# Pruned attention: five of the eight slots of VectorE hand copy 2 to ScalarE

## The chip, the cores and the metric

The kernel runs on one core of one Trainium2 chip. The time is the device time of one execution in microseconds (us), with all inputs in HBM. The core has a matrix engine (TensorE, PE), a vector engine (VectorE, DVE), a scalar engine (ScalarE, ACT), a general one (GpSimd, POOL) and one that here only issues DMAs (SyncE, SP). Each runs its own instructions in the order in which they are written; they meet through semaphores only.

## What is computed

A decoder of two layers on 8 sequences of 512 tokens with 256 features. Of its six parts the change concerns one, the cross-attention of layer 0, with 16 heads of 16 features. Its columns of scores are pruned: for each head the probabilities are summed over the queries, and only the 460 key positions with the largest sums are kept.

```python
scores = jnp.einsum('bhqd,bhkd->bhqk', q, k) / math.sqrt(D_K)
scores = jax.nn.softmax(scores, axis=-1)
keep = int(S * PRUNE_KEEP)
col_sum = jnp.sum(scores, axis=2)
_, idx = jax.lax.top_k(col_sum, keep)
mask = jnp.zeros((B, H, S), scores.dtype).at[jnp.arange(B)[:, None, None], jnp.arange(H)[None, :, None], idx].set(1.0)
pruned = scores * mask[:, :, None, :]
return jnp.einsum('bhqk,bhkd->bhqd', pruned, v)
```

## The kernel before

The program is a sequence of stages; `stage_xattn0` is the pruned attention. It goes through 8 batches `b`, each in two halves `u` of 8 heads, and through a half in 8 slots `h` = 0 to 7, one head in each (`slots`). Batches 0 and 1 are written out, batches 2 to 7 are a loop, so that each engine jumps back five times; a last pass (b = 8) ends the pipeline. Heads are counted by `n`.

In slot `h` of head n the engines do this, in the order of their code:

- PE: transposes 0 of head n-2 (`turn`, L911), the second half of the scores of head n (`scores`, L903), transposes 1, then what the slot has besides (value products of the half before in slots 0 to 5, L892; output projection in slots 6 and 7 of halves with u = 1, L957; the turned column sums in slot 3, L940), transposes 2, the first half of the scores of head n+1, transposes 3.
- DVE: the maximum of score rows for two of the four row tiles (`maxima`, L795), the reciprocal of the row sums of head n-1 (L791), the maxima of the other two, its copies, and between them the search for the 52 smallest column sums of the half before. The search has 16 steps (`search`: L808, L818, L826, L811), three in each of slots 3 to 7 and one more in slot 7, and works on 8 partitions, one per head. In slot 0 DVE prunes the values (`xa_vm`, L855), in slots 0 to 2 with u = 0 it does the layer norm of an earlier batch (L832 to L840 and L879).
- ACT: copy 0 of head n-2, two exponentials with row sums (L764), copy 1, two more exponentials, copy 3. In slot 6 it first copies a result, `xa_oT` (L772).
- POOL: the normalisation of head n (L746), four operations, after the reciprocal.

A copy (`turned`, L668 to L681) takes one transposed 128 x 512 tile of probabilities from PSUM (`xa_ps_t`) to SBUF (`xa_probT`) and sums it along its row, which gives the column sum. A head has four tiles t = 0 to 3. `by_vector` says which engine copies tile t in slot h: DVE on L679 with a `tensor_scalar`, ACT on L681 with an `activation`, each with an accumulator as second output, read by an instruction of its own. Before, DVE has tile 2 in all slots and tile 3 in slot 1: 9 of 32 copies in a half.

PSUM has two buffers for transposes, `ps_t[t % 2]`. So `turn` makes PE wait until an earlier copy has freed one: transposes 2 and 3 wait for copies 0 and 1 of the same slot, transposes 0 and 1 for copies 2 and 3 of the slot before.

Of the kernel before, what the change touches and what calls it, by code (L numbers as in the profile page):

```python
# [56 lines left out]
def wait(eng, sem, count):  # L57

    if not isinstance(count, int) or count > 0:
        eng.wait_ge(sem, count)  # L60
# [520 lines left out]
def stage_xattn0(nc, a):  # L581
# [16 lines left out]
    with ExitStack() as ctx:  # L598
# [38 lines left out]
        def since(b, first):  # L637
            return not isinstance(b, int) or b >= first

        def batches(eng, body):  # L640

            body(0)
            body(1)
            with eng.Fori(2, B) as b:
                body(b)
            body(B)

        def slots(b):
            for u in range(2):
                for h in range(HU):  # L650
                    yield u, h, HU * u + h, 2 * HU * b + HU * u + h, not isinstance(b, int) or b < B
# [5 lines left out]
        def has_before2(b, u):  # L657
            return not isinstance(b, int) or 2 <= 2 * b + u <= 2 * B + 1

        def by_vector(h, t):  # L660

            return t == 2 or (t == 3 and h == 1)

        def turning(b, u, h, n, real):

# [92 lines left out]
        @block.scalar  # L758
        def _(act):
            def body(b):  # L760
                def exponentials(h, n, j):
                    act.wait_ge(max_up, 2 * n + j + 1)
                    for t in (2 * j, 2 * j + 1):
                        ins = act.activation(probs[h % NP][:, t, :], ps_s[j][:, t % 2, :], ACT.Exp,  # L764
                                             bias=nmax[h % 2][:, t:t + 1], accum_out=rsum[h % 2][:, t:t + 1])
                    ins.then_inc(exp_up, 1)

                for u, h, hh, n, real in slots(b):
                    if h == 6 and has_before2(b, u):
                        act.wait_ge(vals_up, 2 * b + u - 1)  # L770
                        wait(act, y_up, 2 * (b - 1))
                        act.activation(oT[:, u, :], ps_v[:, :], ACT.Copy).then_inc(oT_up, 1)  # L772
                    turned(act, b, u, h, n, real, 0)
                    if real:
                        wait(act, t_up, 4 * (n - 3))
                        exponentials(h, n, 0)
                    turned(act, b, u, h, n, real, 1)
                    if real:
                        exponentials(h, n, 1)
                    if not by_vector(h, 3):  # L780
                        turned(act, b, u, h, n, real, 3)
            batches(act, body)

        @block.vector
        def _(dve):
# [56 lines left out]
            def body(b):  # L842
                for u, h, hh, n, real in slots(b):
                    if real:
                        maxima(n, h, 0)
                    search(b, u, h, (0,))
                    if (real or (u, h) == (0, 0)) and not (isinstance(b, int) and n == 0):
                        reciprocal(n - 1, h - 1)
                    if real:
                        maxima(n, h, 1)  # L850
                    if h == 0 and has_before2(b, u):
                        dve.wait_ge(kept_up, 2 * b + u - 1)
                        dve.wait_ge(v_ld[u], 16 * b)
                        for q4 in range(2):
                            ins = dve.tensor_tensor(vm[:, :, q4, :, q4 * DK:(q4 + 1) * DK],  # L855
                                                    v[u][:, :, q4 * QH * DK:(q4 + 1) * QH * DK].rearrange("p t (j d) -> p t j d", d=DK),
                                                    ps_m[:, 0:T * HU].rearrange("p (t q j o) -> p t q j o", t=T, q=2, o=1)[:, :, q4, :, :]
                                                    .to_broadcast([P, T, QH, DK]), ALU.mult)
                        ins.then_inc(vm_up, 1)
                    search(b, u, h, (1,))  # L860
                    turned(dve, b, u, h, n, real, 2)
                    if by_vector(h, 3):
                        turned(dve, b, u, h, n, real, 3)
                    search(b, u, h, (2, 3) if h == HU - 1 else (2,))
                    if u == 1 and h in (6, 7) and since(b, 1):
                        i = h - 6
                        dve.wait_ge(y_up, 2 * b - 1 + i)
                        dve.wait_ge(xb_up, b)
                        dve.tensor_tensor(x_in[:, 2 * i:2 * i + 2, :], ps_m[:, :].rearrange("p (t d) -> p t d", t=2),
                                          x_in[:, 2 * i:2 * i + 2, :], ALU.add).then_inc(add_up, 1)  # L870
                    if (u, h) == (0, 0) and since(b, 2):
                        stats(b - 2)
                    if (u, h) == (0, 2) and since(b, 2):
                        finish(b - 2)
# [1545 lines left out]
```

## Time and profile before

| | us |
|---|---|
| time, median of 3 runs (2188.01 to 2202.6) | 2197.36 |
| the profiled execution's own time | 2182.38 |
| its span, first to last instruction | 2180.6 |
| PE busy in the span | 1880.1 (86%) |
| DVE busy | 1300.3 (60%) |
| ACT busy | 959.1 (44%) |
| POOL busy | 609.9 (28%) |

The profile is that of one execution. A row of a timeline has the start of an instruction in us from the span's start, how long it lasted, engine, line, operation and operands; in brackets stands the idle time of the engine before it and what ended it ("issue": nothing that the profile shows). Rows of one engine can overlap a little at their ends, so the time that an operation occupies is read from the start of it to the start of the next one, when the engine does not wait between. The pruned attention lies between about 325 and 1010 us.

### The profile page before, as it was taken

What the parts mean: (1) busy time and instruction counts of PE and PEld (TensorE: products, weight loads), DVE (VectorE), ACT (ScalarE), POOL (GpSimd) and SP (SyncE); (2) the same over time, 40 slices, a digit from 0 to 9 for tenths busy, and PEclk for the clock granted to TensorE, in tenths of its full rate; (3) what the DMA queues carried; (4) which work ended last, traced back from release to release, by engine and by line L of the source; (5) the groups of instructions that cost most, each with busy time, mean ns of one, the idle gap of its engine ahead of it and who ended that gap; (6) DMA issues with size and microseconds to landing.
All of it is one profiled execution on the core that took longest, in us unless ns stands there. A gap on an engine that the chain in (4) does not pass through costs nothing. (4 is left out here: it accounts for less than half of the span.)

```text
span 2180.6 us, 28641 instructions
## 1 busy us (share of the span) xinstructions
PE 1880.1 (86%) x8625; PEld 1134.5 (52%) x8625; DVE 1300.3 (60%) x3113; ACT 959.1 (44%) x2451; POOL 609.9 (28%) x781
## 2 busy tenths in 40 slices
PE   7794857888888888884697899999879999999997
PEld 5452534444554454551565565666555656566553
DVE  2483437988988988983354121122266677766655
ACT  3231549988888888880232211111123232223220
POOL 2010005555555555551355000100143122211100
PEclk9897988999999999997666999999999999999999
DMA  5523752112112112202622333433321121100000
GB/s 193 231 87 99 248 183 65 46 54 67 56 54 66 55 54 60 61 20 73 203 92 91 98 109 132 138 123 130 107 77 59 34 63 44 30 15 25 10 10 20
DMA packets 166839, 184.51 MB, mean 85 GB/s; under 512 B 19620, under 2 KB 145819, under 8 KB 165696
## 3 DMA queue, kind: packets, MB, share of 16 engines
q1 hardware_dynamic: 159424, 158.57, 22.5%
q0 software_dynamic: 6144, 16.18, 2.4%
q10 hardware_dynamic: 1152, 8.39, 0.9%
q8 instruction: 48, 0.79, 0.2%
q14 instruction: 71, 0.58, 0.1%
HBM read 118.68 MB, written 58.72 MB: 81 GB/s over the span
## 5 line engine op out<-in xcount | busy, mean ns | idle before, releaser
L746 POOL TENSOR_SCALAR xa_probs<-xa_probs,xa_rinv 128x512 f32<-128x512 f32 x512 | 344.6, 692 | 294.6 <-DVE xa_rinv L791 294.6
L911 PE MATMUL xa_ps_t<-xa_ident,xa_probs 128*128 128x128 f32 x2048 | 325.7, 285 | 60.8 <-POOL xa_probs L746 55.0
L764 ACT ACTIVATE xa_probs<-xa_ps_s,xa_nmax 128x512 f32<-128x512 f32 x512 | 351.9, 708 | 25.8 <-DVE xa_nmax L795 25.4
L911 PEld LDWEIGHTS xa_ps_t<-xa_ident,xa_probs 128*128 128x128 f32 x2048 | 232.4, 143 | 240.1 <-POOL xa_probs L746 84.7
L795 DVE TENSOR_REDUCE xa_nmax<-xa_ps_s 128x2 f32<-128x1024 f32 x256 | 307.3, 1201 | 39.5 <-PE xa_ps_s L903 38.0
L681 ACT ACTIVATE xa_probT<-xa_ps_t 128x512 f32<-128x512 f32 x368 | 226.5, 621 | 63.0 <-PE xa_ps_t L911 54.1
L2268 PE MATMUL ta_ps_e<-k_ew,ta_x5T 128*128 128x512 f32 x512 | 244.2, 613 | 1.5 <-DVE ta_acc L2018 1.4
L903 PE MATMUL xa_ps_s<-xa_k,xa_q 96*128 96x512 bf16 x512 | 157.8, 391 | 54.9 <-ACT xa_probs L764 34.5
L2018 DVE SCALAR_TENSOR_TENSOR ta_acc<-ta_ps_e,ta_gate,ta_acc 128x256 f32<-128x256 f32 x256 | 123.5, 482 | 101.7 <-PE ta_ps_e L2268 95.5
L1459 ACT ACTIVATE ex_hid<-ex_ps_g 128x512 f32<-128x512 f32 x64 | 38.2, 598 | 274.1 <-PE ex_ps_u L1561 274.1
L1515 DVE TENSOR_TENSOR ex_hid<-ex_hid,ex_ps_u 128x512 f32<-128x512 f32 x64 | 44.0, 687 | 182.0 <-ACT ex_hid L1459 182.0
L2268 PEld LDWEIGHTS ta_ps_e<-k_ew,ta_x5T 128*128 128x128 f32 x512 | 98.4, 197 | 102.7 <-issue 86.5
L892 PE MATMUL xa_ps_v<-xa_probT,xa_vm 128*32 128x512 f32 x1024 | 135.2, 619 | 0.8 <-DVE xa_vm L855 0.8
L679 DVE TENSOR_SCALAR_CACHE_REDUCE xa_probT<-xa_ps_t 128x512 f32<-128x512 f32 x144 | 97.7, 679 | 41.4 <-PE xa_ps_t L911 40.0
L1561 PE MATMUL ex_ps_g<-ex_xsT,k_wg 128*128 128x512 f32 x256 | 120.4, 592 | 2.1 <-ACT ex_xsT L1441 2.1
L1561 PE MATMUL ex_ps_u<-ex_xsT,k_wu 128*128 128x512 f32 x256 | 120.3, 592 | 0.0
L764 ACT ACTIVATION_READ_ACCUMULATOR xa_probs<-xa_ps_s,xa_nmax 128x1 f32 x512 | 116.7, 228 | 0.0
L1571 PE MATMUL ex_ps_d<-k_wd,ex_hid 128*128 128x256 f32 x512 | 113.4, 379 | 0.1
L1571 PEld LDWEIGHTS ex_ps_d<-k_wd,ex_hid 128*128 128x128 f32 x512 | 96.0, 190 | 13.3 <-DVE ex_hid L1515 0.5
L903 PEld LDWEIGHTS xa_ps_s<-xa_k,xa_q 96*128 96x128 bf16 x512 | 45.0, 100 | 77.2 <-ACT xa_probs L764 49.8
L681 ACT ACTIVATION_READ_ACCUMULATOR xa_probT<-xa_ps_t 128x1 f32 x368 | 84.7, 230 | 0.0
L1183 POOL DMA_INDIRECT scratch_buf<-ro_xs,ro_pi x64 | 63.0, 984 | 67.8 <-issue 67.8
(356 smaller groups left out, 2935.2 us busy)
## 6 DMA issues: line engine op xcount, KB each, us to landing
xa_q<-scratch_qk_parts SPq DMA_DIRECT2D x192, 64.0 KB, 2.2
xa_k<-scratch_qk_parts SPq DMA_DIRECT2D x192, 64.0 KB, 2.2
scratch_buf<-rec_zeros ACTq DMA_DIRECT2D x8, 1024.0 KB, 12.0
k_wg<-in_L_ffn_Wg SPq DMA_DIRECT2D x16, 512.0 KB, 5.8
k_wu<-in_L_ffn_Wu SPq DMA_DIRECT2D x16, 512.0 KB, 6.0
k_wd<-in_L_ffn_Wd SPq DMA_DIRECT2D x16, 512.0 KB, 6.7
ex_xs<-scratch_buf SPq DMA_DIRECT2D x16, 512.0 KB, 4.9
scratch_results<-ex_out SPq DMA_DIRECT2D x16, 512.0 KB, 3.3
```

The source lines that it names most:

```text
L679: eng.tensor_scalar(dst, src, 1.0, 0.0, ALU.mult, ALU.add, accum_out=out).then_inc(copied[t], 1)
L681: eng.activation(dst, src, ACT.Copy, accum_out=out).then_inc(copied[t], 1)
L746: ins = pool.tensor_scalar(probs[h % NP][:, t, :], probs[h % NP][:, t, :], rinv[h % 2][:, t:t + 1], 1.0, ALU.mult, ALU.mult)
L764: ins = act.activation(probs[h % NP][:, t, :], ps_s[j][:, t % 2, :], ACT.Exp, bias=nmax[h % 2][:, t:t + 1], accum_out=rsum[h % 2][:, t:t + 1])
L795: dve.tensor_reduce(nmax[h % 2][:, 2 * j:2 * j + 2], ps_s[j][:, :, :], AX.X, ALU.max, negate=True).then_inc(max_up, 1)
L892: ins = pe.matmul(ps_v[32 * j:32 * j + 32, :], vm[:, t, four, j, :], probT[u][:, QH * four + j, t, :], start=(four == 0 and t == 0), stop= ...
L903: ins = pe.matmul(ps_s[j][:, t % 2, :], q[c % 2][:, hh % CH, t * P:(t + 1) * P], k[c % 2][:, hh % CH, :], start=True, stop=True)
L911: ins = pe.transpose(ps_t[t % 2][:, i * P:(i + 1) * P], probs[(h - 2) % NP][:, i, t * P:(t + 1) * P], ident[:, :])
L1561: ins = pe.matmul(ps[:, :], wt[:, h, j * P:(j + 1) * P], xsT[u][:, h, :], start=(h == 0), stop=(h == DH - 1))
L1571: ins = pe.matmul(ps_d[:, t, :], hid[u][:, j, t * P:(t + 1) * P], wd[u][:, j, :], start=(j == 0), stop=(j == FT - 1))
L2018: dve.scalar_tensor_tensor(acc[c % 2][:, t, :], ps_e[n % 2][:, i, :], gate[c % 2][:, t, e:e + 1], acc[c % 2][:, t, :], ALU.mult, ALU.add). ...
L2268: ins = pe.matmul(ps_e[n % 2][:, :, :].rearrange("p e d -> p (e d)"), x5T[c % 2][:, h, t * P:(t + 1) * P], ew[:, h, e:e + 2, :].rearrange( ...
```

## The change

`by_vector` gets another rule: DVE copies tile 2 in slots 0, 1 and 2, and tile 3 in slots 1 and 2, which are 5 of 32 copies in a half; ACT copies the other 27. In code, both engines now ask the rule for tiles 2 and 3 at the places where their copies 2 and 3 stood. All arithmetic and all buffers stay.

```diff
--- before.py
+++ after.py
@@ -659,7 +659,7 @@
 
         def by_vector(h, t):
 
-            return t == 2 or (t == 3 and h == 1)
+            return h < 3 and (t == 2 or (t == 3 and h > 0))
 
         def turning(b, u, h, n, real):
 
@@ -777,8 +777,9 @@
                     turned(act, b, u, h, n, real, 1)
                     if real:
                         exponentials(h, n, 1)
-                    if not by_vector(h, 3):
-                        turned(act, b, u, h, n, real, 3)
+                    for t in (2, 3):
+                        if not by_vector(h, t):
+                            turned(act, b, u, h, n, real, t)
             batches(act, body)
 
         @block.vector
@@ -858,9 +859,9 @@
                                                     .to_broadcast([P, T, QH, DK]), ALU.mult)
                         ins.then_inc(vm_up, 1)
                     search(b, u, h, (1,))
-                    turned(dve, b, u, h, n, real, 2)
-                    if by_vector(h, 3):
-                        turned(dve, b, u, h, n, real, 3)
+                    for t in (2, 3):
+                        if by_vector(h, t):
+                            turned(dve, b, u, h, n, real, t)
                     search(b, u, h, (2, 3) if h == HU - 1 else (2,))
                     if u == 1 and h in (6, 7) and since(b, 1):
                         i = h - 6
```

On ACT, the excerpt runs from slot 5 to slot 7 of a half with an `xa_oT` copy (names: `xa_probT` the copies, `xa_probs` the exponentials). Before:

```order
L764 ACTIVATE xa_probs,xa_rsum<-xa_ps_s,xa_nmax 128x512 x2
L681 ACTIVATE xa_probT,xa_colsum<-xa_ps_t 128x512
L772 ACTIVATE xa_oT<-xa_ps_v 128x512
L681 ACTIVATE xa_probT,xa_colsum<-xa_ps_t 128x512
L764 ACTIVATE xa_probs,xa_rsum<-xa_ps_s,xa_nmax 128x512 x2
L681 ACTIVATE xa_probT,xa_colsum<-xa_ps_t 128x512
L764 ACTIVATE xa_probs,xa_rsum<-xa_ps_s,xa_nmax 128x512 x2
L681 ACTIVATE xa_probT,xa_colsum<-xa_ps_t 128x512 x2
L764 ACTIVATE xa_probs,xa_rsum<-xa_ps_s,xa_nmax 128x512 x2
```

The same place in the changed kernel:

```order
L764 ACTIVATE xa_probs,xa_rsum<-xa_ps_s,xa_nmax 128x512 x2
L681 ACTIVATE xa_probT,xa_colsum<-xa_ps_t 128x512 x2
L772 ACTIVATE xa_oT<-xa_ps_v 128x512
L681 ACTIVATE xa_probT,xa_colsum<-xa_ps_t 128x512
L764 ACTIVATE xa_probs,xa_rsum<-xa_ps_s,xa_nmax 128x512 x2
L681 ACTIVATE xa_probT,xa_colsum<-xa_ps_t 128x512
L764 ACTIVATE xa_probs,xa_rsum<-xa_ps_s,xa_nmax 128x512 x2
L681 ACTIVATE xa_probT,xa_colsum<-xa_ps_t 128x512 x3
L764 ACTIVATE xa_probs,xa_rsum<-xa_ps_s,xa_nmax 128x512 x2
```

The two copies in a row (3, then 0 of the next slot) have become three (2, 3, then 0), and the one before `xa_oT` has become two.

On DVE, the excerpt runs from the copies of slot 1 to the search step after the copy of slot 3 (L795 and L796 are maxima, L791 and L792 reciprocals, `xa_left` and `xa_m` the search). Before:

```order
L679 TENSOR_SCALAR xa_probT,xa_colsum<-xa_ps_t 128x512 x2
L795 TENSOR_REDUCE xa_nmax<-xa_ps_s 128x2
L791 RECIPROCAL xa_rinv<-xa_rsum 128x4
L795 TENSOR_REDUCE xa_nmax<-xa_ps_s 128x2
L679 TENSOR_SCALAR xa_probT,xa_colsum<-xa_ps_t 128x512
L795 TENSOR_REDUCE xa_nmax<-xa_ps_s 128x2
L808 TENSOR_SCALAR xa_left<-xa_ps_m 8x512
L791 RECIPROCAL xa_rinv<-xa_rsum 128x4
L795 TENSOR_REDUCE xa_nmax<-xa_ps_s 128x2
L818 MAX xa_m<-xa_left 8x8
L679 TENSOR_SCALAR xa_probT,xa_colsum<-xa_ps_t 128x512
L826 MATCH_REPLACE xa_left<-xa_m,xa_left 8x512
```

And in the changed kernel:

```order
L679 TENSOR_SCALAR xa_probT,xa_colsum<-xa_ps_t 128x512 x2
L796 TENSOR_REDUCE xa_nmax<-xa_ps_s 128x2
L792 RECIPROCAL xa_rinv<-xa_rsum 128x4
L796 TENSOR_REDUCE xa_nmax<-xa_ps_s 128x2
L679 TENSOR_SCALAR xa_probT,xa_colsum<-xa_ps_t 128x512 x2
L796 TENSOR_REDUCE xa_nmax<-xa_ps_s 128x2
L809 TENSOR_SCALAR xa_left<-xa_ps_m 8x512
L792 RECIPROCAL xa_rinv<-xa_rsum 128x4
L796 TENSOR_REDUCE xa_nmax<-xa_ps_s 128x2
L819 MAX xa_m<-xa_left 8x8
L827 MATCH_REPLACE xa_left<-xa_m,xa_left 8x512
```

Slot 2 has two copies instead of one, and the copy between the search steps of slot 3 is gone, as it is in slots 4 to 7.

## Rows read from the trace of the kernel before

**Rows 1.** The page's 40 slices of 54.5 us: busy share in tenths.
```profile
DVE  2483437988988988983354121122266677766655
ACT  3231549988888888880232211111123232223220
```

**Rows 2.** Windows: busy us (count) of PE, PEld, DVE, ACT, POOL; PEclk; DMA.
```profile
380.00:390.00 10.00, 8.14 (x43) 5.67 (x44) 10.00 (x21) 9.27 (x30) 5.38 (x8) 0.83 0.11 33
640.00:720.00 80.00, 68.67 (x469) 38.73 (x468) 72.75 (x147) 69.96 (x217) 45.16 (x65) 1.00 0.20 60
```

**Rows 3.** The page's costliest groups: count | busy us, mean ns | idle before.
```profile
L681 ACT ACTIVATE xa_probT<-xa_ps_t 128x512 f32<-128x512 f32 x368 | 226.5, 621 | 63.0 <-PE xa_ps_t L911 54.1
...
L679 DVE TENSOR_SCALAR_CACHE_REDUCE xa_probT<-xa_ps_t 128x512 f32<-128x512 f32 x144 | 97.7, 679 | 41.4 <-PE xa_ps_t L911 40.0
```

**Rows 4.** Timeline of ACT, slots 4 to 7 of a half with u=1.
```profile
707.55 0.60 ACT L681 ACTIVATE xa_probT<-xa_ps_t 128x512 f32<-128x512 f32 x1 [0.47 <-PE xa_ps_t L911]
...
712.55 0.60 ACT L681 ACTIVATE xa_probT<-xa_ps_t 128x512 f32<-128x512 f32 x1 [0.48 <-PE xa_ps_t L911]
...
716.93 0.63 ACT L772 ACTIVATE xa_oT<-xa_ps_v 128x512 f32<-128x512 f32 x1
717.40 0.64 ACT L681 ACTIVATE xa_probT<-xa_ps_t 128x512 f32<-128x512 f32 x1
...
724.62 0.59 ACT L681 ACTIVATE xa_probT<-xa_ps_t 128x512 f32<-128x512 f32 x1
...
726.51 0.61 ACT L681 ACTIVATE xa_probT<-xa_ps_t 128x512 f32<-128x512 f32 x1
...
728.83 0.60 ACT L681 ACTIVATE xa_probT<-xa_ps_t 128x512 f32<-128x512 f32 x1 [1.61 <-issue]
```

**Rows 5.** Timeline of PE, the same slots: transposes after POOL and after ACT.
```profile
711.86 0.66 PE L911 MATMUL xa_ps_t<-xa_ident,xa_probs 128*128 128x128 f32 x4 [1.00 <-POOL xa_probs L746]
...
725.35 0.66 PE L911 MATMUL xa_ps_t<-xa_ident,xa_probs 128*128 128x128 f32 x4 [0.39 <-ACT xa_probT L681]
```

**Rows 6.** Timeline of DVE: slots 1, 2 and 4 with u=0; slot 3 with u=1.
```profile
655.03 0.69 DVE L679 TENSOR_SCALAR_CACHE_REDUCE xa_probT<-xa_ps_t 128x512 f32<-128x512 f32 x1 [1.00 <-PE xa_ps_t L911]
...
655.90 0.69 DVE L679 TENSOR_SCALAR_CACHE_REDUCE xa_probT<-xa_ps_t 128x512 f32<-128x512 f32 x1 [0.17 <-PE xa_ps_t L911]
...
660.55 1.38 DVE L879 TENSOR_SCALAR xa_x_in<-xa_x_in,xa_mv,xa_rstd 128x256 f32<-128x256 f32 x4
...
666.64 1.20 DVE L795 TENSOR_REDUCE xa_nmax<-xa_ps_s 128x2 f32<-128x1024 f32 x1
...
670.22 0.67 DVE L679 TENSOR_SCALAR_CACHE_REDUCE xa_probT<-xa_ps_t 128x512 f32<-128x512 f32 x1
...
670.83 0.68 DVE L818 MAX8 xa_m<-xa_left 8x8 f32<-8x512 f32 x1
671.43 1.19 DVE L795 TENSOR_REDUCE xa_nmax<-xa_ps_s 128x2 f32<-128x1024 f32 x1
...
703.14 0.68 DVE L808 TENSOR_SCALAR xa_left<-xa_ps_m 8x512 f32<-8x512 f32 x1 [0.88 <-PE xa_ps_m L940]
```

**Rows 7.** Timeline of ACT, a half with u=0, and slot 0 after it.
```profile
663.10 0.69 ACT L764 ACTIVATE xa_probs<-xa_ps_s,xa_nmax 128x512 f32<-128x512 f32 x1 [0.52 <-DVE xa_nmax L795]
...
667.38 0.60 ACT L681 ACTIVATE xa_probT<-xa_ps_t 128x512 f32<-128x512 f32 x1 [0.34 <-PE xa_ps_t L911]
...
686.65 0.60 ACT L681 ACTIVATE xa_probT<-xa_ps_t 128x512 f32<-128x512 f32 x1 [0.33 <-PE xa_ps_t L911]
...
687.85 0.69 ACT L764 ACTIVATE xa_probs<-xa_ps_s,xa_nmax 128x512 f32<-128x512 f32 x1 [0.52 <-DVE xa_nmax L795]
```

**Rows 8.** Timeline of ACT in the stage's first half: slots 6 and 7.
```profile
353.11 0.74 ACT L681 ACTIVATE xa_probT<-xa_ps_t 128x512 f32<-128x512 f32 x1
...
353.68 0.84 ACT L764 ACTIVATE xa_probs<-xa_ps_s,xa_nmax 128x512 f32<-128x512 f32 x1
...
358.04 0.89 ACT L764 ACTIVATE xa_probs<-xa_ps_s,xa_nmax 128x512 f32<-128x512 f32 x1
```

## The prediction

> **What bounds the kernel now.** I read the slices first: VectorE (DVE) and ScalarE (ACT) are both at eight or nine tenths from slice 8 to 18 [rows 1]. That is the pruned attention, and nothing outside it is touched. The windows view of 80 us in its middle has DVE busy 72.8, ACT 70.0 and TensorE (PE) 68.7 us [rows 2]: three engines near their limit, so sums over the stage decide nothing, and the timeline has to be read slot by slot (a slot is one head; "slot 3" is h = 3).
>
> In slots 3 to 7 DVE has no idle time. Its first maximum of one slot starts at 666.64 and that of the next at 671.43, 4.79 us later, and the copy between them is handed over without a gap (copy at 670.22, search step at 670.83) [rows 6]. ACT runs after it: from copy 0 of slot 4 (707.55) to that of slot 5 (712.55) it needs 5.00 us, of which 0.48 is idle time before the copy, ended by PE's transposes [rows 4], which had themselves waited 1.00 us for GpSimd (POOL), and this for DVE's reciprocal [rows 5]. With no search, as in the stage's first half, the same seven ACT operations repeat after 4.36 us (353.68 to 358.04) [rows 8]. So in slots 3 to 7 DVE sets a pace of 4.79, and ACT could do 4.36.
>
> **Prices of one operation.** A copy on ACT, back to back with what follows, occupies 0.57 us (353.11 to 353.68) [rows 8], though such a row lasts 0.60 and more; so an exponential is (4.36 - 3 x 0.57) / 4 = 0.66 [rows 8]. A copy on DVE occupies 0.61 (670.22 to 670.83) [rows 6]. A copy is thus equally dear on both, and only place and order matter.
>
> **What the change moves.** In slots 3 to 7 copy 2 goes from DVE to ACT, in slot 2 copy 3 goes the other way: net 4 of 32 per half, 64 in the 16 halves, so ACT's 368 copies become 432 and DVE's 144 become 80 [rows 3]. Nothing is removed or added; PE, POOL and the DMA queues keep their order.
>
> *Slots 3 to 7, DVE.* 4.79 - 0.61 = 4.18 us of work: no longer the limit.
>
> *Slots 3 to 7, ACT.* Four exponentials and four copies: 4 x 0.66 + 4 x 0.57 = 4.92 us, already over 4.79. Then comes a wait that is new. PE writes transposes 0 and 2 of a head into the same PSUM buffer, so the next slot's transposes 0 wait for copy 2. Copy 2 is now ACT's last but one operation. An ACT copy releases PE 0.73 after its start (copy at 724.62 [rows 4], transposes waiting for it at 725.35 [rows 5]), and ACT starts a copy 0.69 after its transposes start (711.86 [rows 5] to 712.55 [rows 4]): 1.42 us from copy 2 to the next copy 0, while copies 2 and 3 fill 1.14. So 0.28 us of idle time, and a slot of **5.20 us**. Queued behind copy 0 are the exponentials, for which DVE's reciprocal and POOL wait; they had some 1.9 us to spare, as DVE now comes to the reciprocal early.
>
> *From copy 0 of slot 4 to copy 0 of slot 0.* Half with u = 0: 667.38 to 686.65, 19.27 us [rows 7]. After: four slots of 5.20, and in slot 6 the copy of oT (0.47: 716.93 to 717.40 [rows 4]), which covers the 0.28, so +0.20: 21.0. **+1.7**. Half with u = 1: 707.55 to 728.83, 21.28 us [rows 4]. After: 5.20 + 5.40 + 5.20 and a last slot of 4.92 plus what ACT needs from the start of its last copy to the new loop pass, less that copy's own 0.57 (2.32 - 0.57 = 1.75; "issue", 726.51 to 728.83 [rows 4]), which hides the 0.28: 22.5. **+1.2**.
>
> *Slot 3.* DVE has to do copy 3 of slot 2 before the first maximum of slot 3. Two copies in a row start 0.87 apart (655.03, 655.90), since PE has to turn in between; so DVE is free 0.87 later than at 660.55 [rows 6]. In a half with u = 0 this delays the exponential of 663.10, which waits for the maximum, to 663.97 [rows 7]; 3.21 later (four exponentials and a copy) copy 2 starts, 1.42 later the next copy 0: 668.60 instead of 667.38. **+1.2**. With u = 1 DVE has 0.88 idle at 703.14 for the column sums [rows 6], which takes this up; there the sum is **+0.3** (the same working without the four DVE operations of L879 in front). What ACT saves in slot 2 (0.57) ends in this wait.
>
> *Slot 0 after a half with u = 0.* ACT waited 0.52 for a maximum (687.85), DVE being late from its search [rows 7]. Gone: **-0.6**, with the propagation.
>
> Slots 0 to 2 otherwise stay: PE is full there with the value matmuls.
>
> **The sum.** Per batch 1.7 + 1.2 + 1.2 + 0.3 - 0.6 = 3.8. Batches 1 to 7: 26.6, less 0.9 because batch 1 has no L879 in front. First half of batch 0, ACT-bound at 4.36: 5 x (5.20 - 4.36) = 4.2. Second half of batch 0: about 1.5. Together **+31 us**. The profiled execution took 2182.4, so 2213; it lies below all three timed ones (2188.0 to 2202.6), so against their median of 2197.4 I predict **2228 us**. What a measurement of this kernel can tell from no change is about 1%, 22 us.
>
> **A page against the trace.** The rows give 0.57 per ACT copy with its accumulator [rows 8]. The Trainium skill, page "ScalarE: Activation LUTs", section "What ACT_TABLE_LOAD costs", gives an ACTIVATE with immediate scale 186 ns + 0.833 ns per element and lets neighbours overlap by about 93 ns: an estimate of 0.52 for 512 elements. By that, four copies would take 0.2 less per slot, and the time would grow by about 15 us instead of 31. The trace disagrees, and the measured 0.57 stands; that formula has no accumulator read-out. The same page's section "Rules for kernel authors" sends multiplications to VectorE, not ScalarE, for its speed in bf16; these are fp32 tiles in PSUM, and the rows show 0.61 against 0.57.
>
> **The rivals.**
>
> *The 0.28 wait does not come* (PE turns sooner than its rows say, or runs ahead). Slots of 4.92: seven waits of 0.28 fewer per batch, 13.7, and 2.8 in batch 0: +15, 2212. For it: PE has over 1 us to spare in these slots. Against: the 1.42 is made of two measured steps with no slack in them. Chance 0.14.
>
> *Copies in a row are cheaper on ACT.* The oT copy, which reads no accumulator, occupies 0.47 [rows 4]. If the three copies in a row went at that pitch, a slot would be 4 x 0.66 + 4 x 0.47 = 4.52 plus a wait of 1.42 - 0.94 = 0.48, so 5.00 for 5.20: 0.2 less in 5 x 16 slots, +15, again 2212. Chance 0.05. (The Trainium skill's formula above points this way.)
>
> *Faster.* Only if that pitch held and the wait were gone too would ACT's 4.52 beat the 4.79 of now, by 0.27 x 5 x 15 = 20 us: 2177. It decides below a slot of 4.79. Against both: copies 3 and 0 already run back to back in the first half, at 4.36 per slot [rows 8], which leaves no such saving. Chance 0.04.
>
> *PE's clock.* It is granted 1.00 from 640 to 720 with PE busy 0.86, but 0.83 from 380 to 390, where PE is busy 0.81 [rows 2]. Slots of 5.20 leave PE idle more. If each of the 14 later halves lost one further 1 us to a spell at the lower level (1.2 GHz), the time would be 2242. It points the same way as the forecast. Chance 0.15.
>
> *The forecast:* ACT takes over as the bound, 0.28 wait included. Chance 0.62.
>
> **How the numbers follow.** Slower by over 1% means above 2219: the forecast and the clock (0.77), less a little for the spread of the runs: 0.75. Within 1%: the first two rivals (0.19), which may also end a little above: 0.20. Faster: 0.05. The range goes from 2207 (first rival, less 5 for spread) to 2246 (clock, plus 4).
>
> **What would show it.** ACT: in slots 3 to 6 copy 0 starts every 5.20, with 0.2 to 0.3 idle before it, ended by PE, and PE's transposes waiting there for ACT's copy instead of POOL. DVE: idle before its second maximum, and 80 copies. Stage about 31 us longer, nothing else moved. Wrong if slots 4 to 7 repeat in 4.9 or less, if DVE still has no gaps there, or if the loss sits in slots 0 to 2.

## The result and the profile after

The changed kernel took 2257.98 us in the median (2249.07 to 2265.07), the kernel before 2193.01 us beside it: a ratio of 1.0297, 95% interval 1.0252 to 1.0341. It is slower by 65 us, where 31 were predicted.

The page of the changed kernel, its slices and the groups that answer to [rows 1] and [rows 3]:

```profile
PE   7785857788787888786389699999978999999997
...
DVE  2482436877777787777144212122256776666655
ACT  3232648988887888885033211111113322223220
...
PEclk9897978998999999999676699999989999999999
...
L764 ACT ACTIVATE xa_probs<-xa_ps_s,xa_nmax 128x512 f32<-128x512 f32 x512 | 349.8, 700 | 43.9 <-DVE xa_nmax L796 43.7
L681 ACT ACTIVATE xa_probT<-xa_ps_t 128x512 f32<-128x512 f32 x432 | 261.7, 618 | 69.6 <-PE xa_ps_t L912 68.8
...
L679 DVE TENSOR_SCALAR_CACHE_REDUCE xa_probT<-xa_ps_t 128x512 f32<-128x512 f32 x80 | 55.1, 690 | 47.7 <-PE xa_ps_t L912 47.7
```

ACT has its 432 copies and DVE its 80, as counted. DVE's eights and nines of before are sevens, ACT's stayed at eight: nobody is full, and yet it takes longer. Over 420 to 1000 us the windows view has PE (the first number after the stretch's length) busy for less time than before, and a lower granted clock (the third number from the end). Before, and then in the changed kernel:

```profile
420.00:1000.00 580.00, 492.74 (x3326) 280.27 (x3326) 521.86 (x1060) 492.02 (x1513) 318.88 (x452) 0.98 0.18 55
...
420.00:1000.00 580.00, 470.87 (x3049) 269.69 (x3048) 460.01 (x862) 492.99 (x1522) 294.50 (x421) 0.94 0.17 53
```

The span grew from 2180.6 to 2252.9 us. From the first exponential of the stage to its last one it is 647.5 us before and 713.9 after (327.18 to 974.68, and 328.43 to 1042.31): 66 of the 72 us lie there.

The timeline of ACT in slots 3 to 5 of a half with u = 0, which answers to [rows 4]:

```profile
705.98 0.62 ACT L681 ACTIVATE xa_probT<-xa_ps_t 128x512 f32<-128x512 f32 x1
...
706.55 0.63 ACT L681 ACTIVATE xa_probT<-xa_ps_t 128x512 f32<-128x512 f32 x1
...
707.50 0.60 ACT L681 ACTIVATE xa_probT<-xa_ps_t 128x512 f32<-128x512 f32 x1 [0.23 <-PE xa_ps_t L912]
...
711.30 0.62 ACT L681 ACTIVATE xa_probT<-xa_ps_t 128x512 f32<-128x512 f32 x1
...
712.82 0.60 ACT L681 ACTIVATE xa_probT<-xa_ps_t 128x512 f32<-128x512 f32 x1 [0.23 <-PE xa_ps_t L912]
```

and PE at the same place:

```profile
706.83 0.63 PE L912 MATMUL xa_ps_t<-xa_ident,xa_probs 128*128 128x128 f32 x4 [1.35 <-ACT xa_probT L681]
```

The mechanism is the predicted one. Copy 2 starts at 705.98, copy 3 at 706.55, PE's next transposes have waited 1.35 us for ACT and not for POOL, and copy 0 comes at 707.50; the next pair is 711.30 and 712.82. From copy 2 to copy 0 it is 1.52 us, where 1.42 was predicted, and a slot takes 5.33 (707.50 to 712.82) and not 5.20.

But look at the loop end, where DVE's operations of [rows 6] would have followed each other without a gap:

```profile
770.17 0.67 DVE L870 TENSOR_TENSOR xa_x_in<-xa_ps_m,xa_x_in 128x512 f32<-128x512 f32 x1
773.44 1.23 DVE L796 TENSOR_REDUCE xa_nmax<-xa_ps_s 128x2 f32<-128x1024 f32 x1 [2.60 <-issue]
775.75 0.18 DVE L792 RECIPROCAL xa_rinv<-xa_rsum 128x4 f32<-128x4 f32 x1 [1.08 <-issue]
```

ACT at the same place:

```profile
771.47 0.60 ACT L681 ACTIVATE xa_probT<-xa_ps_t 128x512 f32<-128x512 f32 x1 [0.17 <-PE xa_ps_t L912]
...
774.70 0.69 ACT L764 ACTIVATE xa_probs<-xa_ps_s,xa_nmax 128x512 f32<-128x512 f32 x1 [2.55 <-DVE xa_nmax L796]
...
777.11 0.69 ACT L764 ACTIVATE xa_probs<-xa_ps_s,xa_nmax 128x512 f32<-128x512 f32 x1 [0.38 <-DVE xa_nmax L796]
```

and PE (L893 are the value products):

```profile
776.20 0.61 PE L904 MATMUL xa_ps_s<-xa_k,xa_q 96*128 96x512 bf16 x2 [2.98 <-ACT xa_probs L764]
...
777.86 1.93 PE L893 MATMUL xa_ps_v<-xa_probT,xa_vm 128*32 128x512 f32 x8 [0.37 <-DVE xa_vm L856]
```

DVE stands still for 2.60 us and again for 1.08, and the profile shows nothing that it waits for. ACT waits 2.55 us for DVE's maximum, PE 2.98 us for ACT, and eight value products take 1.93 us in place of the 1.06 that they take otherwise: after this idle time the granted clock falls (0.57 from 777 to 781 us). The prediction had no such row: before, it was ACT that stood still at this place, 1.61 us [rows 4]. The waits view of DVE from 680 to 960 us lists four of each, one pair at each loop end.

For the rest of this text a **step** is the time from the first exponential of one slot to that of the next, read from ACT's timeline. These are the steps of batch 5, which is in the loop; the last one of the second row crosses the loop end. "Placed" is the changed kernel with DVE's code moved (below), "early" ACT's copy 2 between the exponentials.

| | h = 0 | 1 | 2 | 3 | 4 | 5 | 6 | 7 | sum |
|---|---|---|---|---|---|---|---|---|---|
| before, u = 0 | 5.70 | 5.01 | 5.04 | 4.86 | 4.79 | 4.85 | 4.78 | 5.47 | 40.5 |
| before, u = 1 | 4.94 | 5.76 | 4.36 | 5.22 | 5.01 | 4.83 | 5.30 | 6.27 | 41.7 |
| changed, u = 0 | 6.91 | 5.60 | 5.93 | 5.33 | 5.58 | 5.41 | 5.39 | 5.33 | 45.5 |
| changed, u = 1 | 4.93 | 5.77 | 4.64 | 5.33 | 5.33 | 5.40 | 5.39 | 7.94 | 44.7 |
| changed, placed, u = 0 | 5.60 | 5.10 | 5.92 | 5.34 | 5.33 | 5.41 | 5.86 | 5.33 | 43.9 |
| changed, placed, u = 1 | 4.94 | 5.77 | 4.63 | 5.34 | 5.33 | 5.41 | 5.41 | 5.27 | 42.1 |
| slots 3 to 7 only, early, u = 0 | 5.56 | 5.30 | 5.03 | 4.94 | 4.93 | 5.40 | 5.30 | 4.93 | 41.4 |
| slots 3 to 7 only, early, u = 1 | 4.99 | 5.77 | 4.35 | 5.23 | 5.01 | 5.40 | 4.92 | 4.96 | 40.6 |

The changed kernel has three kinds of loss: slots 3 to 6 at 5.3 to 5.4 and slot 2 at 5.9 or 4.6, which were predicted; 7.94 and 6.91 around the loop end, which were not; and single steps in other halves, such as 7.22 and 7.18 in slot 0 of batches 1 and 2 with u = 1, where 4.94 is usual. They turn out to be the clock's.

### The profile page after: what moved, and what is told of

The parts are those of the page before. It is cut to its first block and busy times, and to the rows that moved or that the text cites. A ratio compares the mean times of both kernels' runs of the same rounds, so it can differ in the third digit from the quotient of the medians.

```text
span 2252.9 us, 28641 instructions
## 1 busy us (share of the span) xinstructions
PE 1905.7 (85%) x8625; PEld 1158.6 (51%) x8625; DVE 1275.0 (57%) x2985; ACT 999.4 (44%) x2579; POOL 609.9 (27%) x781
## 5 line engine op out<-in xcount | busy, mean ns | idle before, releaser
L912 PE MATMUL xa_ps_t<-xa_ident,xa_probs 128*128 128x128 f32 x2048 | 338.0, 295 | 96.5 <-ACT xa_probT L681 95.3
L912 PEld LDWEIGHTS xa_ps_t<-xa_ident,xa_probs 128*128 128x128 f32 x2048 | 247.1, 149 | 279.1 <-issue 159.7
L796 DVE TENSOR_REDUCE xa_nmax<-xa_ps_s 128x2 f32<-128x1024 f32 x256 | 310.6, 1214 | 112.0 <-PE xa_ps_s L904 96.5
L764 ACT ACTIVATE xa_probs<-xa_ps_s,xa_nmax 128x512 f32<-128x512 f32 x512 | 349.8, 700 | 43.9 <-DVE xa_nmax L796 43.7
L681 ACT ACTIVATE xa_probT<-xa_ps_t 128x512 f32<-128x512 f32 x432 | 261.7, 618 | 69.6 <-PE xa_ps_t L912 68.8
L904 PE MATMUL xa_ps_s<-xa_k,xa_q 96*128 96x512 bf16 x512 | 167.8, 412 | 61.6 <-ACT xa_probs L764 41.5
L893 PE MATMUL xa_ps_v<-xa_probT,xa_vm 128*32 128x512 f32 x1024 | 141.9, 647 | 2.6 <-DVE xa_vm L856 2.6
L681 ACT ACTIVATION_READ_ACCUMULATOR xa_probT<-xa_ps_t 128x1 f32 x432 | 97.9, 227 | 0.0
L679 DVE TENSOR_SCALAR_CACHE_REDUCE xa_probT<-xa_ps_t 128x512 f32<-128x512 f32 x80 | 55.1, 690 | 47.7 <-PE xa_ps_t L912 47.7
```

The lines of the kernel that those rows point to most:

```text
L681: eng.activation(dst, src, ACT.Copy, accum_out=out).then_inc(copied[t], 1)
L796: dve.tensor_reduce(nmax[h % 2][:, 2 * j:2 * j + 2], ps_s[j][:, :, :], AX.X, ALU.max, negate=True).then_inc(max_up, 1)
L893: ins = pe.matmul(ps_v[32 * j:32 * j + 32, :], vm[:, t, four, j, :], probT[u][:, QH * four + j, t, :], start=(four == 0 and t == 0), stop= ...
L904: ins = pe.matmul(ps_s[j][:, t % 2, :], q[c % 2][:, hh % CH, t * P:(t + 1) * P], k[c % 2][:, hh % CH, :], start=True, stop=True)
L912: ins = pe.transpose(ps_t[t % 2][:, i * P:(i + 1) * P], probs[(h - 2) % NP][:, i, t * P:(t + 1) * P], ident[:, :])
```

## The experiments

Ratios are to the kernel before, run beside each.

### The loop end

**DVE without a loop, in the changed kernel.**

```diff
-            batches(dve, body)
+            for b in range(B + 1):
+                body(b)
             stats(B - 1)
```

> The changed kernel, but with VectorE's part of the pruned attention written out for all batches instead of looped from batch 2; the other engines keep their loops, and every operation and its order stay. Theory A (the relief of VectorE uncovers its own loop jump: 2.60 us of VectorE idle at each loop end of the changed kernel, 0 before, and PE's clock falls after it): the jump goes, the step from slot 7 to slot 0 falls from 7.9 to about 5.6 us and the one after it from 6.9 to about 5.6, some 3.5 us for each of 5 loop ends, so 17 us less than the changed kernel, a ratio to the kernel before of about 1.022. Rival B (that idle time is only where some other engine's jump shows): no change, ratio 1.029 to 1.030.

Measured: 2232.11 us, ratio 1.0188 (1.0150 to 1.0225), so some 24 us less than the changed kernel, where 17 were expected. The step across the loop end fell from 7.9 to 5.26, the next from 6.9 to 5.55. The loss at the loop end is DVE's.

**The same in the kernel before.**

> The kernel before with the same edit, as the control. Theory A: VectorE's jump was covered by its backlog of queued work, so nothing is gained: ratio 0.998 to 1.002. Rival B2 (written-out code is quicker for reasons of its own, or slower to fetch): a change like that of the other kernel, some 15 us in either direction.

Measured: 2192.03 us, ratio 0.9992 (0.9967 to 1.0016). Written-out code gains nothing as such. Up to here my theory was that DVE always lost this time at the jump and had hidden it behind its backlog.

**Only slots 3 to 7 moved,** slot 2 as before.

```diff
-            return h < 3 and (t == 2 or (t == 3 and h > 0))
+            return h < 3 and (t == 2 or (t == 3 and h == 1))
```

> Only the first part of the change: copy 2 to ScalarE in slots 3 to 7; copy 3 of slot 2 stays on ScalarE. Theory (VectorE's extra copy in slot 2 delays the first maximum of slot 3 by 0.9 us where the layer norm's four operations stand before it, little elsewhere): about 1 us less per batch than the changed kernel, 6 to 8 us, a ratio of about 1.026. Rival (the extra copy is covered by PE, which is full there): ratio as the changed kernel's, 1.029 to 1.030, or above it as ScalarE has 0.57 more to do.

Measured: 2224.52 us, ratio 1.0149 (1.0112 to 1.0186): 33 us less than the changed kernel, where 6 to 8 were expected, and this is what overthrew the theory. Slot 2 gave its 0.9 (5.03 for 5.93), but the loop end also went from 7.9 to 5.27, and DVE's waits "issue" were gone, though its loop was still a loop and it had even less to do. The view of the DMA queues told why. From 680 to 960 us the changed kernel has on its instruction queue

```profile
q1 hardware_dynamic: 18285, 14.46, 17.0%
q14 instruction: 17, 0.14, 0.2%
```

17 fetches of 8 KB (0.14 MB over 17), and the kernel before

```profile
q1 hardware_dynamic: 19344, 15.22, 18.2%
q14 instruction: 16, 0.13, 0.2%
```

16 of them. Four of the changed kernel's fall at each loop end, and one in mid-pass. The kernel with slots 3 to 7 moved has none at all. So some loops are not fetched again after their first pass, and some are fetched anew in each. In the kernel before it was ACT's loop; in the changed one, whose two loops have other lengths and starts, ACT's stays and DVE's does not.

**DVE's loop moved by 16 instructions,** in the changed kernel. The 16 memsets go to a tile of their own and are executed once, while DVE waits for the stage to begin.

```diff
+            for i in range(16):
+                dve.memset(spare[:, i:i + 1], 0.0)
             dve.wait_ge(pad_up, 1)
```

> The changed kernel with 16 tiny VectorE memsets into an unused tile at the start of the pruned attention, before VectorE's loop; nothing in the loop is changed. In the changed kernel four 8 KB fetches of instructions fall at each loop end and one in mid-pass, and VectorE stands idle for them; in the one with only slots 3 to 7 moved there is none at all, though VectorE has as much idle time. Theory P (whether VectorE's loop stays in its instruction buffer depends on where its code lies, not on how busy it is): shifting the loop by 16 instructions takes it out of the bad place: no fetches in the loop, steps from slot 7 to 0 of 5.3 instead of 7.9 and from 0 to 1 of 5.6 instead of 6.9, ratio about 1.019. Theory A (the loop jump shows because VectorE has no backlog): no change, 1.029.

Measured: 2236.24 us, ratio 1.0179 (1.0114 to 1.0244). Sixteen instructions more, and 26 us less than the changed kernel (1.0297 - 1.0179). The size is loose: the two intervals allow 9 to 43 us, and the medians differ by 22. The traces are sharper. The two steps around a loop end take 10.88 us together at each of the five, where the changed kernel takes 14.8 to 15.1: 20 us in all, and the stage from its first to its last exponential is 24 us shorter (689.9 for 713.9). Its queues from 680 to 960 us; there is no row for an instruction queue:

```profile
## 3 DMA queue, kind: packets, MB, share of 16 engines
q1 hardware_dynamic: 19872, 16.00, 18.7%
issues: line engine op xcount, KB each, median us to landing
```

**By 64, and by 128.** Each was executed once.

> The same with 64 memsets. Theory P: fetches in the loop either there or not, depending on the place; with both this and the one of 16 unlike the changed kernel, place is the cause. Theory A: the same fetches and the same idle time of 2.6 us at each loop end as in the changed kernel, a time of about 2258.

> The changed kernel with 128 memsets ahead of VectorE's loop, which is 8 KB of instructions at 64 bytes each, the size of one fetch. Theory P128 (what counts is where in such a block the loop begins and ends): the place is as bad as in the changed kernel: fetches in the loop, 15 to 17 of them from 680 to 960, steps of 7.9 and 6.9 at the loop end, and a time of about 2258. Rival (the place counts in some other way, by distance from something else): no fetches, 2232 to 2238, as with 16 and 64.

With 64: 2232.54 us, no fetches, steps of 5.27 across the loop end. With 128: 2250.72 us, and the queues again have

```profile
q1 hardware_dynamic: 18207, 14.40, 17.2%
q14 instruction: 17, 0.14, 0.2%
```

with DVE idle for its maximum four times and for its reciprocal four times:

```profile
DVE xa_nmax L799 <- issue: 10.4, 4, 2.7
DVE xa_rinv L795 <- issue: 4.4, 4, 1.1
```

Over the whole span this kernel has one packet more on that queue than the changed kernel (73 for 72), so 128 instructions are about the 8 KB of one fetch. A shift by 16 or 64 cures, a shift by 128 restores the fault, steps of 7.9 and 6.9 included. These three shifts fit the reading that what decides is where the loop's code lies within such a block; other shifts were not tried. The Trainium skill, page "Runtime: NRT & Kernel Launch", section "Instruction fetch mechanics", describes a small instruction buffer that is refilled in order, and a stall where a jump's target is not in it. The trace agrees with the stall, 2.60 us of it in DVE's row at 773.44; the page's refill unit is 16 KB, while the packets here are of 8 KB, and 8 KB is the shift that brings the fault back. (A second instruction queue, q8, does have packets of 16 KB: 48 packets, 0.79 MB in every run; in the changed kernel none of them falls from 600 to 960 us.) Which start and which length are bad was not worked out.

**ACT's loop moved by 40 instructions,** in the kernel before.

```diff
+            for i in range(40):
+                apart(act, past_act)
```

> The kernel before with 40 semaphore increments put ahead of ScalarE's first pass of the pruned attention; its loop is unchanged, only moved. In the kernel before, ScalarE stands idle 1.6 to 1.8 us at each loop end and 16 fetches of instructions fall in the stretch from 680 to 960. Theory P (place of a loop in the instruction stream decides on fetches, on this engine too): if the new place is a good one, no fetch in that stretch and 0.9 us less per loop end, the rest being covered by VectorE's backlog: 4 to 5 us less, ratio 0.998. If nothing changes, either the place is bad too or the theory does not hold for ScalarE.

Measured: 2187.06 us, ratio 0.9981 (0.9960 to 1.0002). The fetches are gone,

```profile
## 3 DMA queue, kind: packets, MB, share of 16 engines
q1 hardware_dynamic: 19344, 15.22, 18.0%
issues: line engine op xcount, KB each, median us to landing
```

and so are ACT's waits "issue", which shows the same for a second engine. The time fell by about 4 us, the size expected, but the interval holds 1, and the trace does not bear out the 0.9 us per loop end. The two steps around a loop end take 11.84 us together at each of the five, and in the kernel before they take 11.83 or 11.84 at three of them, with ACT's fetches there: DVE's load is the bound, and the fetches cost nothing. The other two took 12.77 and 12.06 before, with the granted clock at 0.73 and 0.72 just after; whether ACT's fetches had a part in that is not shown.

### The slots

**Copy 2 early.** In the changed kernel, ACT does copy 2 between its last two exponentials (`between()` executes it there, in the slots in which it is ACT's).

```diff
                     for t in (2 * j, 2 * j + 1):
+                        if t == 3:
+                            between()
```

> The changed kernel with ScalarE's copy 2 of slots 3 to 7 done between the last two exponentials instead of after them, so that two operations lie between it and the next copy 0 instead of one. Theory W (in slots 3 to 7 the pace is ScalarE's work of 4.92 us plus a wait for PE, which waited for copy 2): slots fall from 5.33 to about 4.92 to 4.95, 0.4 in 7 slots of each of 8 batches, about 23 us less than the changed kernel, a ratio of about 1.019; if the shorter slots uncover other waits, less. Rival (the wait is bound by something else, such as the clock or the reciprocal): slots stay above 5.2 and the ratio above 1.026.

Measured: 2227.37 us, ratio 1.0161 (1.0125 to 1.0196). ACT's timeline in slots 3 and 4:

```profile
690.01 0.67 ACT L681 ACTIVATE xa_probT<-xa_ps_t 128x512 f32<-128x512 f32 x1
...
690.58 0.77 ACT L766 ACTIVATE xa_probs<-xa_ps_s,xa_nmax 128x512 f32<-128x512 f32 x1
...
691.24 0.68 ACT L681 ACTIVATE xa_probT<-xa_ps_t 128x512 f32<-128x512 f32 x1
...
691.81 0.69 ACT L681 ACTIVATE xa_probT<-xa_ps_t 128x512 f32<-128x512 f32 x1
...
692.38 0.79 ACT L766 ACTIVATE xa_probs<-xa_ps_s,xa_nmax 128x512 f32<-128x512 f32 x1
```

Copy 2 at 690.01, an exponential, copies 3 and 0 at 691.24 and 691.81 without a gap. PE's transposes, waiting for copy 2, start

```profile
690.91 0.63 PE L917 MATMUL xa_ps_t<-xa_ident,xa_probs 128*128 128x128 f32 x4 [0.68 <-ACT xa_probT L681]
```

0.90 after it, and their result is there when ACT comes to it. Slots 3, 4, 6 and 7 mostly fell to 4.93 to 4.95 (4.92 by ACT's work alone; 5.01 in slot 4 with u = 1). So 0.4 us of each of these slots was this wait. The step of slot 5, in which the copy to `xa_oT` stands between copy 2 and the next copy 0, stayed at 5.41: there the wait had been covered, as predicted. The total fell by 30 us where 23 were expected; the time at the lower clock fell too, from 66 to 41 us between 420 and 1000. The loop end kept its 7.9, DVE's code being that of the changed kernel.

**Copy 2 early and slot 2 as before.** This is the kernel with only slots 3 to 7 moved, with the copy between the exponentials; neither loop is fetched anew.

> Copy 2 to ScalarE in slots 3 to 7 as in the change, but placed between the last two exponentials, and slot 2 left as before. By ScalarE's work alone: slots of 4.93 and one of 5.41 against 4.79 to 5.0 before, no wait for copy 2, no extra copy ahead of slot 3, and no fetches in the loop (both loops lie as in the kernel with only slots 3 to 7 moved). Per batch about 1.0 more than before in slots 3 to 7 and 0.9 less at the loop end: ratio 0.999 to 1.004. If the overload of ScalarE costs more than its own work says, 1.008 or above.

Measured: 2189.18 us, ratio 0.9982 (0.9964 to 1.0000). ACT's waits from 420 to 960 us in this kernel:

```profile
ACT xa_probT L681 <- PE xa_ps_t L917: 26.3, 26, 1.9
ACT xa_probs L766 <- DVE xa_nmax L801: 5.4, 12, 0.5
```

and in the changed kernel, for the same stretch:

```profile
ACT xa_probT L681 <- PE xa_ps_t L912: 50.0, 77, 3.1
ACT xa_probs L764 <- DVE xa_nmax L796: 29.6, 24, 2.7
```

All of the move to ACT in slots 3 to 7, and no loss, also against the kernel before with ACT's loop moved (0.9981), which likewise fetches neither loop anew. The overload of ACT as such (4.92 against 4.79 in a slot) is paid back in halves with u = 1 (40.6 for 41.7), where DVE was the slower one.

**Slot 2 alone:** copy 3 of slot 2 to DVE, the rest as before.

```diff
+            return t == 2 or (t == 3 and h in (1, 2))
```

> Only the second part of the change: copy 3 of slot 2 goes to VectorE, while copy 2 of slots 3 to 7 stays there. Working from the slot steps: with u = 0 the first maximum of slot 3 comes 0.87 us later and, VectorE being without gaps until slot 7, that delay is not made up: about 0.9 per batch; with u = 1 some 0.3. So 8 us, ratio 1.003 to 1.005, if the loop fetches stay as before; up to 20 us more (1.013) if VectorE's loop falls in the bad place, 8 less if ScalarE's leaves it.

Measured: 2204.33 us, ratio 1.0061 (1.0030 to 1.0093), 13 us where 8 were expected: the 0.9 of slot 2 (5.92 for 5.03) with u = 0 and 0.3 (4.64 for 4.36) with u = 1 as expected, and beyond that five steps of 6.76 to 6.87 in slot 0, which are the matter of the next part.

### The clock

**PE kept busy, slots 3 to 7 moved.**

```diff
-                        scores(b, hh + 1, n + 1, 0)
+                        scores(b, hh + 1, n + 1, 0, 2 if h > 2 and not (u == 1 and h > 5) else 1)
```

> The kernel with only slots 3 to 7 moved (ratio 1.0149), in which PE computes the first half of the next head's scores twice in slots 3 to 7, except slots 6 and 7 with u = 1: 0.43 us more PE work in 8 of 16 slots, in time that PE spends waiting for ScalarE's copy 2. The result is the same. Theory C (part of the loss is PE at 1.2 instead of 2.4 GHz after it idled in these slots: 59 us at the lower clock there, 21 before): the low spells become fewer, steps of 6.7 to 6.8 at slots 0 fall to 4.9 to 5.6, and the time falls by 5 to 8 us, ratio 1.011 to 1.013, in spite of the added work. Rival (the low spells come on their own, or cost nothing): the spells stay at 50 us or more, and the ratio at 1.015 or above.

Measured: 2213.32 us, ratio 1.0092 (1.0059 to 1.0125), 12 us less than without the added matmuls, where 5 to 8 were expected. In the traces, 34 us between 341 and 1000 us are at the lower clock where it was 59. But the expected cure of the steps did not come: three of them take 7.00 to 7.18 where three took 6.69 to 6.80, and the stage of this one trace is only 1.3 us shorter. So the gain rests on the totals and on the clock that each timed execution lists: its mean is 0.927 to 0.936 in the eight with the added matmuls, and 0.920 to 0.926 in the four without.

**The same in the changed kernel, DVE's loop moved by 16.**

> The changed kernel moved by 16 instructions (ratio 1.0179, 65 us of the stage at the lower clock), with the first half of the next head's scores computed twice in slots 3 to 7, except slots 6 and 7 with u = 1. Theory C (the rest of the loss beyond the predicted 31 us is the lower clock): low spells fall to 35 us or less, steps of 7.1 to 7.4 in slot 0 of halves with u = 1 become 4.9, the ratio falls by 0.4 to 0.6 points to 1.012 to 1.014, near the 1.014 that the prediction's sum gives. Rival: ratio 1.017 or above.

Measured: 2217.26 us, ratio 1.0114 (1.0074 to 1.0153), and 24 us at the lower clock (341 to 1000 us), against 65 without the added work and 22 in the kernel before. Each of the four steps of 7.1 to 7.4 in slot 0 with u = 1 has become 4.93, one of 6.71 is new (batch 1, u = 0), and the stage is 10 us shorter in the trace. The mean clock is 0.930 to 0.934 in the four executions, 0.916 to 0.921 without. How one of the long steps came about: the windows of the moved kernel before and in such a slot (PE busy is the first number, PEclk the third last):

```profile
697.00:713.00 16.00, 10.53 (x68) 6.00 (x66) 13.03 (x23) 15.54 (x50) 8.05 (x13) 0.99 0.13 39
713.00:719.00 6.00, 6.00 (x27) 3.44 (x26) 3.89 (x7) 4.47 (x14) 3.00 (x6) 0.50 0.27 82
```

and its value products in that slot and later:

```profile
717.46 1.94 PE L896 MATMUL xa_ps_v<-xa_probT,xa_vm 128*32 128x512 f32 x8
...
724.18 1.06 PE L896 MATMUL xa_ps_v<-xa_probT,xa_vm 128*32 128x512 f32 x8
```

With PE busy 10.5 of 16 us in slots 5 to 7, the clock in the six microseconds after is 0.50, the lower level of 1.2 GHz; the value products of slot 0, which then nothing hides, take 1.94 for 1.06, and so do the transposes and scores around them: 2.4 us for one step (7.37 for 4.94). In the kernel with the added matmuls PE is busy 12.3 of 16 us at the same place (11.4 in most other batches, where the clock is 1.00 throughout; here a short spell at the lower clock lies in the stretch, 0.89), and the clock in the slot is 1.00:

```profile
696.00:712.00 16.00, 12.30 (x70) 7.91 (x70) 12.79 (x23) 15.08 (x48) 7.42 (x13) 0.89 0.10 31
712.00:718.00 6.00, 5.68 (x45) 3.22 (x48) 4.61 (x8) 5.59 (x19) 4.56 (x7) 1.00 0.31 93
```

PE does more work there and the kernel is faster. What starts a spell is not settled by this. Without the added work three of the seven halves with u = 1 after batch 0 begin with a step of 4.93 all the same: in each of them a short spell had come a little earlier, in the slots where PE waits anyway (for example PE busy 11.2 of 16 us at a clock of 0.89 before the half at 801.7). A spell costs 2.2 to 2.5 us in such a slot 0 (7.10 to 7.40 for 4.93) and some 0.5 in slot 6 (5.86 for 5.40). From the first exponential to the last one the stage takes 679.8 us, 32 more than before.

### Splits that use both engines

**Slot 4 only, early; slots 4 and 6, early.** Both are the kernel before with these copies moved to ACT and with ACT's loop moved.

> The kernel before, in which ScalarE takes copy 2 in slot 4 alone, between its last two exponentials, with the 40 increments ahead. Theory (VectorE with 4.79 us per slot sets the pace in slots 3 to 7, ScalarE has 0.4 to spare in each): VectorE's five slots fall from 23.95 to 23.35, and ScalarE, with 5 x 4.36 + 0.57 + 0.48 = 22.9, still fits: 0.6 less per half, 9 us over the stage, plus what moving ScalarE's loop gives: ratio 0.993 to 0.996. Rival (any extra copy on ScalarE delays its exponentials and with them PE and GpSimd): ratio 1.000 or above.

> The same with slots 4 and 6, and 32 increments. VectorE's five slots have 22.75 us of work, ScalarE's 5 x 4.36 + 2 x 0.57 + 0.48 = 23.4, so ScalarE becomes the slower: 0.5 less per half than before, about as good as slot 4 alone, ratio 0.993 to 0.997. If the waits of ScalarE for PE come back, 1.000.

Measured: 2187.34 us, ratio 0.9979 (0.9957 to 1.0001), and 2188.76 us, ratio 0.9984 (0.9962 to 1.0005). Both are within their errors of the kernel with ACT's loop moved alone (0.9981), and both missed the 0.993 to 0.997 expected. In slot 4 only, a half with u = 0 takes 40.3 us for 40.5: the copy moved saves 0.2 per half where 0.6 was expected. Copy 2's removal from DVE in slot 4 shows in the step of slot 6 (4.47 for 4.78), but ACT's extra copy costs 0.14 in slot 4 (4.93 for 4.79).

**By half.** ACT takes copy 2 in slots 3 to 7 where u = 1 and in slot 4 where u = 0, early; slot 2 as before; both loops moved.

```diff
+            return (t == 2 and not (u == 1 and h > 2) and not (u == 0 and h == 4)) or (t == 3 and h == 1)
```

> A split by half: with u = 1 ScalarE takes copy 2 in slots 3 to 7, with u = 0 in slot 4 alone, both between the last two exponentials; slot 2 stays as before, both loops moved to places like those without fetches. Where VectorE has two more operations (output added in slots 6 and 7, u = 1), its load is the bound before: the half falls from 41.57 to 40.6; with u = 0 it stays at 40.3. Together 1.1 us per batch, 8 us over the stage, beside the 4 of the fetches: ratio 0.994 to 0.996. Rival (the gains of one half are lost in the next, since the halves are chained): 0.998 as the others.

Measured: 2186.84 us, ratio 0.9966 (0.9943 to 0.9989), where 0.994 to 0.996 was expected. Halves with u = 1 take 40.58 for 41.7, as expected, except three that begin with a step of 6.8; halves with u = 0 take 40.45 for an expected 40.3.

**By half, PE kept busy** in slots 5 to 7 where u = 0.

> The kernel split by half (ratio 0.9966), with the first half of the next head's scores computed twice in slots 5 to 7 of halves with u = 0 only, 24 times in all. Theory C2 (the low spells at slot 0 with u = 1, where three halves take 6.8 instead of 4.94, come from PE's idle time in the three slots before): the three steps of 6.8 fall to 4.94, 5 to 6 us in all, ratio 0.994. Rival (idle time elsewhere causes them, or the doubled work delays VectorE's maxima): ratio 0.997 or above, and steps of 6.8 remain.

Measured: 2179.92 us, ratio 0.9944 (0.9925 to 0.9964). The steps of 6.8 are gone, each is 4.94, and from 341 us to the stage's last exponential (968.6) no spell at the lower clock is left. This one is faster than both kernels, by 12 us (8 to 16) and by 77. What the added matmuls alone gave is less sure: the intervals of 0.9944 and 0.9966 overlap.

## Why the prediction was wrong

The direction was right, the range (2207 to 2246) was not. Step by step:

- **ACT takes over as the bound in slots 3 to 7; PE waits for copy 2: right.** The slot is 5.33 and not 5.20. The term at fault is "an ACT copy releases PE 0.73 after its start": here it was 0.85 (705.98 to 706.83). It is not the neighbour that matters, since with copy 2 early, between two exponentials, it was 0.90 (690.01 to 690.91). The 0.73 had been read at a copy (724.62) that started 1.35 us after ACT had last waited; in the other two places ACT had worked on for 3.2 and 7.5 us without a wait, and its copies last longer in the rows (0.59, 0.62 and 0.67 us). Why the release comes later there is not shown.
- **Slot 3 (+1.2 and +0.3): right.** In the placed kernel the steps of slots 2 and 3 are 1.36 longer with u = 0 (5.92 + 5.34 against 5.04 + 4.86) and 0.39 with u = 1 (4.63 + 5.34 against 4.36 + 5.22).
- **The last slot with u = 1: wrong, in both directions.** I took ACT's 1.61 to 1.8 us of "issue" for a fixed price of its loop jump and carried the 1.75 into the sum, and I gave DVE's jump no term at all. The idle time is the price of fetching the loop anew, and it depends on where the code lies. In the changed kernel ACT no longer paid it, which no term foresaw (21.39 us from copy 0 of slot 4 to copy 0 of slot 0, where 22.5 was forecast), and DVE paid more: the step across the loop end was 7.94, and 5.27 in the placed kernel. That step, a change of code length costed at nothing, failed: 26 us by the placed kernel (1.0297 - 1.0179; 20 us of it read directly at the five loop ends), which is most of the 34 missing. The hint stood in the trace of before: the instruction queue's 16 fetches from 680 to 960 us, in the middle of a loop.
- **The clock: the rival came true beside the forecast, at about its price.** I priced it at 1 us in each of 14 halves, 14 us on top of the forecast (2242 against 2228). The placed kernel with and without PE kept busy differs by 0.65 points, 14 us, with intervals that overlap a little (1.0114 to 1.0244 and 1.0074 to 1.0153); in the kernels with slots 3 to 7 moved it is 12 us (1.0149 and 1.0092, intervals 1.0112 to 1.0186 and 1.0059 to 1.0125). The form was another: not 1 us in every half, but some 2.4 us in a few slots 0. The clock in each timed execution carries the finding more than the totals do. The range, up to 2246, had room for forecast and clock together; what it had no room for is the fetches on top.
- **The sum without these two** is the ratio of the placed kernel with PE kept busy, 1.0114, 25 us (16 to 34), and 32 us in its trace: the 31 predicted agree with both, but partly by luck. In the trace, from copy 0 of slot 4 to copy 0 of slot 0, +1.7 was +2.2 with u = 0, and +1.2 was +0.1 with u = 1, where ACT no longer had the 1.75 and DVE had been the bound before; batch 0, priced at 5.7, lost 8.2. So the slot of 5.33 and the loss in batch 0 on one side and the missing 1.75 on the other cancel. The -0.6 of slot 0 was right (copy 0 to exponential 0.59, where it was 1.20).
- **The rivals.** That the wait would not come was refuted at 707.50. That copies in a row would be cheaper was too, they stay at 0.57 (705.98 to 706.55). The formula of the Trainium skill that spoke for it, from the page "ScalarE: Activation LUTs", section "What ACT_TABLE_LOAD costs", gives 0.52 and stays below the measured pitch when the copy has an accumulator. Nothing was faster in the changed kernel.

What stays open: which places and lengths of a loop are bad; what starts a spell at the lower clock (one fell before a slot 0 of the kernel with slot 4 moved early, after PE had been busy 12.8 of 16 us); and whether a DVE with a backlog would have covered the fetches after its own jump, since no kernel had both.

## What to carry over

Moving work to an engine with idle time is free only if the moved operation does not become the last link before another engine's turn: the same copy one operation earlier cost nothing (0.9982), at the end of the row it cost 0.4 us a slot. When an edit changes how many instructions a looping engine executes, look at the instruction queue's packets inside the loop, before and after; a few neutral instructions ahead of it gave back some 26 of 65 us here. And an engine left idle a little longer, if it is PE, can lose its clock just where its work is not hidden.

## What the runs showed of the hardware that I had not expected

- In these kernels a loop on DVE or ACT is either not fetched at all after its first pass, or fetched anew in each, in packets of 8 KB (17 in 280 us). The same loop moved by 16 or 64 instructions is of the first kind, by 128 of the second. A pass that is fetched anew cost 2.60 and 1.08 us of idle time on DVE, and 1.61 us on ACT, where DVE's load covered it.
- Added matmuls made the kernel faster: some 0.44 us of PE work (two score matmuls, 707.29 to 707.73 in the changed kernel's trace) in 8 of 16 slots took 12 to 14 us off. In the placed kernel the clock then stayed at its level of 2.4 GHz in the slots 0 with u = 1, where PE is the bound.
